# Attention with a running sum moved from PSUM to SBUF, and a third PSUM bank for the scores

## The chip, the cores and the metric

One core of a Trainium2 chip runs the whole program. The metric is the device time of one execution in microseconds; lower is better. The kernel's engines are PE (TensorE), DVE (VectorE), ACT (ScalarE), POOL (GpSimd) and SP, which issues nearly all DMAs.

## What is computed

A transformer block on x of 2 x 2048 tokens with 256 channels: attention with 16 heads of 64, layer norm, a gated network of four layers with 1024 hidden channels, layer norm. The attention is what matters here; it has a normed query and key, a distance bias that a gate on each key scales, and a causal mask.

```python
q = _rmsnorm((x @ Wq).reshape(B, T, H, D), q_rms_w)      # k likewise; v without the norm
gate = softplus(einsum('bthd,hd->bht', k, u_n) / sqrt(D))
bias = -dist * omega_eff[h] * gate[:, :, None, :]        # -inf above the diagonal
scores = einsum('bihd,bjhd->bhij', q, k) / sqrt(D) + bias
y = einsum('bhij,bjhd->bihd', softmax(scores, -1), v).reshape(B, T, H * D) @ Wproj
```

## The kernel before

The attention comes first, for 32 heads (two batches of 16) in 16 pairs; the network's two stages follow and are the same in both kernels. PE multiplies float32 data as rounded float32r, and precision is kept by splitting a value into its rounded part (`_hi`) and the rest (`_lo`), with a product for each part that matters.

For one head, scores are made transposed: keys on the partitions, 512 queries (`QB`) along the columns. A unit is one such tile, 128 keys by up to 512 queries; with four blocks of queries (`qb`, a group each) and the causal mask there are `NU` = 40 units in a head, 4, 8, 12 and 16 for the four groups. For each unit:

- PE makes the scores in a bank of `ps_s` (L1089 and L1090, on the diagonal also L1092, which adds the mask). Banks are taken in turn, two of them; before it, PE waits on `ex_done` for the unit two before (L1084 and L1085).
- ACT takes the exponential out of the bank twice, rounded into `e_hi` (L757, not for whole units) and full into `e_all` (L764). `e_all` has a ring of 3 and is overwritten when POOL's rest of the unit three before is made.
- POOL makes `e_lo` = `e_all` - `e_hi` (`take_rest`, L489) for the split units ("P"); units of mode "F", 14 of the 40, are multiplied whole.
- PE multiplies with the values, two units late (`LAG`; L1110 for a whole unit, L1115, or L1120 and L1122, for a split one) and four units late with `e_lo` (`LAG_LO`; L1131). The output is a bank of `ps_v`, which ACT copies out at the end of a group (L773).

L1115 serves the units called merged: `kt` even and not on the diagonal, 12 in a head (2, 4 and 6 in the groups `qb` 1, 2 and 3). One matmul with 128 columns of stationary data gives the products of `e_hi` with the rounded values, the sum of the weights, and the rests of the values but for the last column's, for which there is no room. That column is made on DVE: for each merged unit it multiplies `e_hi` with the column's rests, one scalar per key, and adds to a running sum in the PSUM bank `ps_r`. L993 starts the sum, L995 goes on, L999 ends it into `last_rest` (SBUF, rounded, two buffers in turn), and once a group PE adds this with the matmul L1109 (`to_last` picks the column). DVE's L998 waits until PE is through with the group two before, that is with that buffer's reader.

Row maxima for the softmax come from a product of their own: PE writes a tile of queries by keys into one of two banks `ps_m` (L1070), 40 in a head, and DVE reduces it (L957 on the diagonal, which also adds the mask, and L960 elsewhere); PE waits for the max two before (`mx_free`). DVE also has the norms, gates and the low part of transposed queries and keys (L946); POOL has squares and the splits of weights and values.

The bank `ps_r` has a second use ahead of the sums: `work_bank` lets the projections, the root's scratch and the transposes of the first head alternate between `ps_p` and `ps_r`, and `first_bank` takes it as one of four for the first transposes of x.

The order of the work on every engine is one list, `attention_steps`, in which each helper step has a due time by hand; every engine goes through the list and executes its part of each step, in order, with semaphores between engines. Heads come in pairs, and in the steady part a pair repeats every 128 us or so.

Of the kernel before, what the change touches and what calls it, by code (L numbers as in the profile page):

```python
# [49 lines left out]
KQ_RING = 2  # L50
E_RING, HI_RING, LO_RING, Q_RING = 3, 4, 3, 3
# [222 lines left out]
def attention(nc, x, wq, wk, wv, q_rms_w, k_rms_w, omega, u, yt_dram, recip_dram, rows_dram, rest_dram, kept, w1_w, w2_w, wproj):  # L274
    ctx = ExitStack()
    with ctx:
# [19 lines left out]
        last_rest = [sb(f"last_rest{i}", [P, QB], F32R) for i in range(2)]  # L296
# [44 lines left out]
        ps_s = [pb(f"ps_s{i}") for i in range(2)]  # L341
# [3 lines left out]
        ps_r = pb("ps_r")  # L345
# [81 lines left out]
        def first_bank(j):  # L427

            return (ps_p, ps_v[0], ps_v[1], ps_r)[j % 4]

        def work_bank(step):
            return (ps_p, ps_r)[work_no[step] % 2] if work_no[step] < two_banks else ps_p
# [268 lines left out]
        def _(act):  # L701
# [6 lines left out]
            for step in steps:  # L708
# [31 lines left out]
                if step[0] == "scores":  # L740
                    n, v = step[1:]
                    u_ = NU * n + v
                    qb, kt = UNITS[v]
                    off = max(0, kt - TQ * qb) * P
                    by = bias[n % 2][:, kt, qb:qb + 1]
                    if v == 0:
                        act.wait_ge(bias_done, n + 1)
                    act.wait_ge(st_full, u_ + 1)
                    if MODES[v] != "F":
                        i = count_of("PD", u_)  # L750
                        if i >= HI_RING:
                            before = split_units[i - HI_RING]
                            act.wait_ge(pv_hi, before + 1)
                            rest_taken(act, before)
                            if merged(before % NU):
                                last_rest_taken(act, before)
                        nc.scalar.activation(e_hi[:, i % HI_RING, off:QB], ps_s[u_ % 2][:, off:QB], ACT.Exp, bias=by).then_inc(hi_done, 1)  # L757
                    if u_ >= E_RING:
                        before = u_ - E_RING
                        if MODES[before % NU] == "F":  # L760
                            act.wait_ge(pv_hi, before + 1)
                        else:
                            rest_taken(act, before)
                    nc.scalar.activation(e_all[:, u_ % E_RING, off:QB], ps_s[u_ % 2][:, off:QB], ACT.Exp, bias=by).then_inc(ex_done, 1)  # L764
# [11 lines left out]
        def _(dve):  # L776
# [70 lines left out]
            for step in steps:  # L847
# [128 lines left out]
                if step[0] == "values":  # L976
# [3 lines left out]
                    if merged(v):  # L980
# [11 lines left out]
                        if kt == 0:  # L992
                            nc.vector.tensor_scalar(ps_r[:], e_in, v_last, None, ALU.mult).then_inc(rest_part, 1)  # L993
                        elif kt < TQ * qb - 2:
                            nc.vector.scalar_tensor_tensor(ps_r[:], e_in, v_last, ps_r[:], ALU.mult, ALU.add).then_inc(rest_part, 1)  # L995
                        else:
                            if grp >= 2:
                                dve.wait_ge(pv_hi, units_before(*divmod(grp - 2, NQB)))  # L998
                            nc.vector.scalar_tensor_tensor(last_rest[grp % 2][:], e_in, v_last, ps_r[:], ALU.mult, ALU.add).then_inc(rest_part, 1)  # L999
# [11 lines left out]
        def _(pe):  # L1011
            pe.wait_ge(s_cg, IDENT_MADE)

            for step in steps:
# [57 lines left out]
                if step[0] == "scores":  # L1072
# [11 lines left out]
                    if u_ >= 2:  # L1084
                        pe.wait_ge(ex_done, u_ - 1)  # L1085
                    out = ps_s[u_ % 2][:, off:QB]
# [4 lines left out]
                    if diag:  # L1091
                        last = nc.tensor.matmul(ps_s[u_ % 2][:, off:off + P], ident_r[:], mask_kq[:], start=False, stop=True)  # L1092
                    last.then_inc(st_full, 1)
                if step[0] == "values":
# [10 lines left out]
                    if MODES[v] == "F":  # L1105
                        pe.wait_ge(ex_done, u_ + 1)
                        if qb and kt == TQ * (qb + 1) - 1:
                            last_rest_taken(pe, NU * n + max(w for w in MERGED if UNITS[w][0] == qb))
                            nc.tensor.matmul(bank[0:D, :], to_last[:], last_rest[grp % 2][:], start=False, stop=False, skip_group_check=True)  # L1109
# [780 lines left out]
```

## Time and profile before

| | us |
|---|---|
| median of 3 runs | 3277.13 (3273.59 to 3280.3) |
| the profiled execution | 3275.87, its span 3274.1 |
| PE busy in the span | 3091.7 (94%) |
| DVE busy | 1842.4 (56%) |
| ACT busy | 1840.9 (56%) |
| POOL busy | 1561.0 (48%) |
| mean granted clock of TensorE | 0.981 of full speed |

A busy time is the union of an engine's instructions; matmuls overlap each other and their ends are modelled, so PE's is not PE at its peak. The shares are over the whole span, of which the attention takes the first 2130 us or so; POOL, DVE and ACT have most of their work there. Times in the rows are from the start of the span. A row of the timeline has the start, the time taken, the engine, line, operation, output and inputs, shape and count; in brackets the idle time before it and what ended that.

### The profile page before, as it was taken

Reading aid. Unit: us, or ns where it says so; the run is one execution under the profiler, and the core shown is the slowest. Engines: PE = TensorE matmul, PEld = TensorE weight load, DVE = VectorE, ACT = ScalarE, POOL = GpSimd, SP = SyncE. Lnnn points to the kernel's source line nnn. Section 1 sums busy time; section 2 is a strip of 40 time slices with the busy share of each in tenths; the row PEclk is TensorE's granted clock in tenths of the full one; section 3 lists DMA queues with packets and bytes.
Section 4 is the critical chain, followed back from the end, with each engine's and each line's share of the span. In section 5 each row is a group of like instructions: output and inputs, shape, how many; then the busy total and the mean of one; then the engine's idle time right before and its main releaser. Section 6 shows DMA issues by size and latency. Waiting matters only on the chain. (4 is left out here: it accounts for less than half of the span.)

```text
span 3274.1 us, 46760 instructions
## 1 busy us (share of the span) xinstructions
PE 3091.7 (94%) x15184; PEld 2404.2 (73%) x15184; DVE 1842.4 (56%) x4184; ACT 1840.9 (56%) x3185; POOL 1561.0 (48%) x1355
## 2 busy tenths in 40 slices
PE   3899999999999999999999999989999999999998
PEld 3667767767667677676776776668888888788887
DVE  6577676676666776766767667653333332232323
ACT  1577777776776777777767777843332332322222
POOL 4476676676665766766766666713222320000000
PEclk7899999999999999999999999989999999999999
DMA  2332432432423324224324235344434443121110
GB/s 70 79 83 51 105 70 65 104 70 64 108 61 92 77 56 105 67 67 104 70 61 111 52 76 146 84 115 133 123 102 116 119 116 116 57 78 39 68 49 20
DMA packets 210355, 273.95 MB, mean 84 GB/s; under 512 B 68992, under 2 KB 96768, under 8 KB 209984
## 3 DMA queue, kind: packets, MB, share of 16 engines
q1 hardware_dynamic: 210112, 270.97, 32.1%
q8 instruction: 121, 1.98, 0.3%
q14 instruction: 122, 1.00, 0.1%
HBM read 97.25 MB, written 55.90 MB: 47 GB/s over the span
## 5 line engine op out<-in xcount | busy, mean ns | idle before, releaser
L489 POOL TENSOR_TENSOR e_lo<-e_all,e_hi 128x512 fp32r<-128x512 f32 (+1 forms) x832 | 1034.4, 1251 | 609.2 <-ACT e_all L764 532.4
L764 ACT ACTIVATE e_all<-ps_s,bias 128x512 f32<-128x512 f32 (+3 forms) x1280 | 786.1, 625 | 168.0 <-PE ps_s L1092 90.6
L757 ACT ACTIVATE e_hi<-ps_s,bias 128x512 fp32r<-128x512 f32 (+1 forms) x832 | 562.0, 676 | 222.5 <-PE ps_s L1090 121.4
L960 DVE TENSOR_REDUCE maxes<-ps_m 128x1 f32<-128x512 f32 x768 | 516.7, 686 | 223.7 <-PE ps_m L1070 221.3
L1070 PE MATMUL ps_m<-k_ext,q_max 128*128 128x512 f32 (+3 forms) x1280 | 460.7, 383 | 55.7 <-issue 17.0
L1089 PE MATMUL ps_s<-q_twice,k_split 128*128 128x512 f32 (+3 forms) x1280 | 485.2, 379 | 25.7 <-ACT e_all L764 20.0
L1090 PE MATMUL ps_s<-q_ext,k_ext 128*128 128x512 f32 (+3 forms) x1280 | 468.9, 366 | 0.0
L1131 PE MATMUL ps_v<-e_lo,v_both 128*65 128x512 f32 (+1 forms) x832 | 432.9, 520 | 21.3 <-POOL e_lo L489 21.3
L1070 PEld LDWEIGHTS ps_m<-k_ext,q_max 128*128 128x128 f32 x1280 | 244.7, 192 | 222.5 <-DVE maxes L957 58.5
L957 DVE CUSTOM_DVE_ANT_0 ps_m<-ps_m,mask_row 128x128 f32<-128x128 f32 (+3 forms) x512 | 253.3, 495 | 245.7 <-PE ps_m L1070 244.1
L1110 PE MATMUL ps_v<-e_all,v_full 128*65 128x512 f32 (+2 forms) x896 | 325.2, 445 | 0.0
L1089 PEld LDWEIGHTS ps_s<-q_twice,k_split 128*128 128x128 f32 x1280 | 242.2, 189 | 107.2 <-ACT e_all L764 73.3
L1090 PEld LDWEIGHTS ps_s<-q_ext,k_ext 128*128 128x128 f32 x1280 | 242.7, 190 | 26.9
L1701 POOL TENSOR_TENSOR dn_rs<-dn_rs,dn_power 128x4 f32<-128x4 f32 x8 | 8.1, 1008 | 461.4 <-DVE dn_rs L1792 461.4
L1732 ACT ACTIVATE dn_gelu<-dn_h,dn_scale 128x512 f32<-128x512 f32 x64 | 44.1, 690 | 321.5 <-PE dn_h L1830 321.5
L727 ACT ACTIVATE raw<-ps_p 128x386 f32<-128x386 f32 x248 | 122.5, 494 | 162.8 <-PE ps_p L1046 161.8
L1415 ACT ACTIVATE gelu<-up_h,up_scale 128x512 f32<-128x512 f32 x64 | 44.1, 689 | 294.9 <-PE up_h L1582 294.9
L1770 DVE TENSOR_TENSOR b_lo<-dn_gelu,b_hi 128x512 fp32r<-128x512 f32 x64 | 44.3, 693 | 288.1 <-ACT b_hi L1736 288.1
L1830 PE MATMUL dn_h<-a_lo,h_hi 128*128 128x512 f32 x512 | 204.2, 399 | 0.0
L1830 PE MATMUL dn_h<-a_hi,h_lo 128*128 128x512 f32 x512 | 204.0, 398 | 0.0
L1582 PE MATMUL up_h<-p_hi,h_hi 128*128 128x512 f32 x512 | 201.8, 394 | 1.4 <-DVE h_lo L1445 1.4
L1830 PE MATMUL dn_h<-a_hi,h_hi 128*128 128x512 f32 x512 | 202.6, 396 | 0.3 <-DVE a_lo L1763 0.3
(230 smaller groups left out, 6569.1 us busy)
## 6 DMA issues: line engine op xcount, KB each, us to landing
q_twice<-q_max SPq DMA_DIRECT2D x256, 128.0 KB, 2.4
yt<-y_out SPq DMA_DIRECT2D x128, 130.0 KB
k_ext<-kq_hi SPq DMA_DIRECT2D x128, 128.0 KB, 2.3
q_max<-kq_hi SPq DMA_DIRECT2D x128, 128.0 KB, 2.4
k_split<-kq_hi SPq DMA_DIRECT2D x128, 128.0 KB, 2.4
k_split<-kq_lo SPq DMA_DIRECT2D x128, 128.0 KB, 2.4
q_ext<-kq_lo SPq DMA_DIRECT2D x128, 128.0 KB, 2.4
hidden<-gelu SPq DMA_DIRECT2D x64, 256.0 KB, 2.1
```

Source lines behind the costliest of these rows:

```text
L489: on.tensor_tensor(e_lo[:, i % LO_RING, off:QB], e_all[:, u_ % E_RING, off:QB], e_hi[:, i % HI_RING, off:QB].bitcast(F32), ALU.subtract).t ...
L757: nc.scalar.activation(e_hi[:, i % HI_RING, off:QB], ps_s[u_ % 2][:, off:QB], ACT.Exp, bias=by).then_inc(hi_done, 1)
L764: nc.scalar.activation(e_all[:, u_ % E_RING, off:QB], ps_s[u_ % 2][:, off:QB], ACT.Exp, bias=by).then_inc(ex_done, 1)
L957: nc.vector.tensor_tensor_reduce(ps_m[m % 2][:, 0:width], ps_m[m % 2][:, 0:width], mask_row[:, QB - width:QB], 1.0, NEG, ALU.add, ALU.max, ...
L960: nc.vector.tensor_reduce(maxes[:, qt, kc:kc + 1], ps_m[m % 2][:, 0:width], AX.X, ALU.max).then_inc(mx_free, 1)
L1070: nc.tensor.matmul(ps_m[m % 2][:, 0:width], q_max[s][:, qt * P:(qt + 1) * P], k_ext[s][:, kc * QB:kc * QB + width], start=True, stop=True) ...
L1089: nc.tensor.matmul(out, k_split[s][:, k], q_twice[grp % Q_RING][:, off:QB], start=True, stop=False)
L1090: last = nc.tensor.matmul(out, k_ext[s][:, k], q_ext[s][:, q], start=False, stop=not diag)
L1110: nc.tensor.matmul(bank[0:V_REST, off:QB], v_full[s][:, kt // TQ, kt % TQ - TQ // 2, 0:V_REST], e_all[:, u_ % E_RING, off:QB], start=False ...
L1131: nc.tensor.matmul(ps_v[(n * NQB + qb) % 2][0:V_REST, off:QB], v_both[s][:, kt, 0:V_REST], e_lo[:, i % LO_RING, off:QB], start=False, stop ...
L1582: last = nc.tensor.matmul(ps_h[o % 2][:], w[:, k, col], p[:, k, :], start=k == 0 and j == 0, stop=k == OC - 1 and j == 2)
L1830: last = nc.tensor.matmul(ps_h[o % 2][:], w[:, k, col], p[:, k, :], start=k == 0 and j == 0, stop=k == OC - 1 and j == 2)
```

## The change

The running sum is in SBUF (`rest_acc`, float32), its last step goes into a single `last_rest`, and the wait ahead of this step is for the group before instead of two before. The PSUM bank that comes free is the third of `ps_s`: `S_RING` = 3, and the scores of a unit wait for the exponential three before. The first uses of `ps_r` as a work bank are now those of `ps_s[2]`, and the scores of unit 2, which take that bank first, wait once for the last turn of head 0.

```diff
+S_RING = 3
-        last_rest = [sb(f"last_rest{i}", [P, QB], F32R) for i in range(2)]
+        rest_acc = sb("rest_acc", [P, QB])
+        last_rest = sb("last_rest", [P, QB], F32R)
-        ps_s = [pb(f"ps_s{i}") for i in range(2)]
+        ps_s = [pb(f"ps_s{i}") for i in range(S_RING)]
-        ps_r = pb("ps_r")
...
-            return (ps_p, ps_r)[work_no[step] % 2] if work_no[step] < two_banks else ps_p
+            return (ps_p, ps_s[2])[work_no[step] % 2] if work_no[step] < two_banks else ps_p
...
                         if kt == 0:
-                            nc.vector.tensor_scalar(ps_r[:], e_in, v_last, None, ALU.mult).then_inc(rest_part, 1)
+                            nc.vector.tensor_scalar(rest_acc[:], e_in, v_last, None, ALU.mult).then_inc(rest_part, 1)
                         elif kt < TQ * qb - 2:
-                            nc.vector.scalar_tensor_tensor(ps_r[:], e_in, v_last, ps_r[:], ALU.mult, ALU.add).then_inc(rest_part, 1)
+                            nc.vector.scalar_tensor_tensor(rest_acc[:], e_in, v_last, rest_acc[:], ALU.mult, ALU.add).then_inc(rest_part, 1)
                         else:
-                            if grp >= 2:
-                                dve.wait_ge(pv_hi, units_before(*divmod(grp - 2, NQB)))
-                            nc.vector.scalar_tensor_tensor(last_rest[grp % 2][:], e_in, v_last, ps_r[:], ALU.mult, ALU.add).then_inc(rest_part, 1)
+                            dve.wait_ge(pv_hi, units_before(*divmod(grp - 1, NQB)))
+                            nc.vector.scalar_tensor_tensor(last_rest[:], e_in, v_last, rest_acc[:], ALU.mult, ALU.add).then_inc(rest_part, 1)
...
-                    if u_ >= 2:
-                        pe.wait_ge(ex_done, u_ - 1)
-                    out = ps_s[u_ % 2][:, off:QB]
+                    if u_ == 2:
+
+                        pe.wait_ge(tr_free, NTURN)
+                    if u_ >= S_RING:
+                        pe.wait_ge(ex_done, u_ + 1 - S_RING)
+                    out = ps_s[u_ % S_RING][:, off:QB]
...
-                            nc.tensor.matmul(bank[0:D, :], to_last[:], last_rest[grp % 2][:], start=False, stop=False, skip_group_check=True)
+                            nc.tensor.matmul(bank[0:D, :], to_last[:], last_rest[:], start=False, stop=False, skip_group_check=True)
```

`first_bank`, both exponentials of ACT (L757, L764) and the mask's matmul (L1092) change in the bank they name alone.

## Rows read from the trace of the kernel before

**Rows 1.** Stretches: us, busy and count per engine, PE's clock, DMA share, GB/s.

```profile
100.00:2130.00 2030.00, 1933.48 (x9399) 1433.28 (x9398) 1398.09 (x3342) 1483.57 (x2626) 1359.38 (x1167) 0.99 0.34 81
```

**Rows 2.** Waits of PE, 100 to 2130 us: total us, times, longest.

```profile
PE ps_v L1131 <- POOL e_lo L489: 21.3, 14, 1.7
PE ps_s L1089 <- ACT e_all L764: 20.0, 49, 0.6
...
PE ps_m L1070 <- DVE maxes L957: 14.8, 17, 1.2
PE ps_m L1070 <- DVE maxes L960: 7.8, 23, 1.1
```

**Rows 3.** Waits of PE's weight loads, 100 to 2130 us, in the same columns.

```profile
PEld ps_s L1089 <- ACT e_all L764: 73.3, 135, 1.0
...
PEld ps_m L1070 <- DVE maxes L957: 54.8, 111, 1.5
...
PEld ps_m L1070 <- DVE maxes L960: 43.0, 106, 1.4
```

**Rows 4.** Timeline, 822 to 840 us: PE's waits late in a pair.

```profile
822.29 0.51 PE L1089 MATMUL ps_s<-q_twice,k_split 128*128 128x512 f32 x1 [0.43 <-ACT e_all L764]
...
836.99 0.50 PE L1089 MATMUL ps_s<-q_twice,k_split 128*128 128x512 f32 x1 [0.55 <-ACT e_all L764]
...
839.71 0.30 PE L1070 MATMUL ps_m<-k_ext,q_max 128*128 128x128 f32 x1 [1.40 <-issue]
```

**Rows 5.** Lines: ns min/median/max, first and last start, forms.

```profile
L946 DVE SCALAR_TENSOR_TENSOR kq_lo<-ps_r,qk_w,kq_hi x2: 750/750/751, 71.5 to 79.5; 128x512 fp32r<-128x512 f32 x2
...
L1089 PE MATMUL ps_s<-q_twice,k_split x1280: 219/393/767, 105.6 to 2128.3; 128*128 128x512 f32 x128, 128*128 128x384 f32 x19, 128*128 128x128 f32 x19, 128*128 128x256 f32 x17
...
L1070 PE MATMUL ps_m<-k_ext,q_max x1280: 220/393/797, 77.4 to 2088.6; 128*128 128x512 f32 x127, 128*128 128x384 f32 x20, 128*128 128x128 f32 x19, 128*128 128x256 f32 x17
```

**Rows 6.** The tile `ps_r`: DVE's sums, in the columns of rows 5.

```profile
L995 DVE SCALAR_TENSOR_TENSOR ps_r<-e_hi,v_both,ps_r x192: 712/747/755, 132.9 to 2124.9; 128x512 f32<-128x512 f32 x192
L993 DVE TENSOR_SCALAR ps_r<-e_hi,v_both x96: 673/747/754, 116.1 to 2111.7; 128x512 f32<-128x512 f32 x96
L999 DVE SCALAR_TENSOR_TENSOR last_rest<-e_hi,v_both,ps_r x96: 736/746/750, 119.6 to 2125.7; 128x512 fp32r<-128x512 f32 x96
```

**Rows 7.** L938 (columns of rows 5), timeline at 2285 us, lines behind 2130 us.

```profile
L938 DVE TENSOR_TENSOR bias<-away,c_all x32: 221/228/585, 70.7 to 2030.4; 128x64 f32<-128x64 f32 x32
...
2284.77 1.30 POOL L1353 TENSOR_TENSOR y_in<-y_in,y_rest 128x512 f32<-128x512 f32 x1 [2.45 <-DMA r_in<-recip_sums]
2285.38 1.23 DVE L1450 TENSOR_TENSOR y_lo<-y_in,y_hi 128x512 fp32r<-128x512 f32 x1 [1.91 <-ACT y_hi L1385]
2286.15 1.62 POOL L1355 TENSOR_TENSOR y_in<-y_in,r_in 128x512 f32<-128x512 f32 x1
...
L1450 DVE TENSOR_TENSOR y_lo<-up_y_first,y_hi 128x512 fp32r<-128x512 f32 x8 | 5.5, 682 | 0.0
```

**Rows 8.** Timeline, 755 to 864 us: sums on DVE, and `e_lo` on POOL.

```profile
755.16 0.74 DVE L999 SCALAR_TENSOR_TENSOR last_rest<-e_hi,v_both,ps_r 128x512 fp32r<-128x512 f32 x1
...
804.72 2.56 POOL L489 TENSOR_TENSOR e_lo<-e_all,e_hi 128x512 fp32r<-128x512 f32 x2
...
806.11 0.75 DVE L995 SCALAR_TENSOR_TENSOR ps_r<-e_hi,v_both,ps_r 128x512 f32<-128x512 f32 x1
...
863.95 0.74 DVE L999 SCALAR_TENSOR_TENSOR last_rest<-e_hi,v_both,ps_r 128x512 fp32r<-128x512 f32 x1
```

**Rows 9.** A wait of ACT, 100 to 2130 us, in the columns of rows 2.

```profile
ACT e_all L764 <- POOL e_lo L489: 69.1, 56, 3.7
```

**Rows 10.** Lines of DVE behind 2130 us: busy us, mean ns; idle before.

```profile
L1779 DVE TENSOR_TENSOR dn_y<-dn_o,dn_scale_out 128x256 f32<-128x256 f32 x32 | 13.6, 423 | 19.5 <-PE dn_o L1842 19.5
L1795 DVE TENSOR_SCALAR dn_y<-dn_y,dn_mean_var,dn_rs 128x256 f32<-128x256 f32 x32 | 11.1, 408 | 9.1 <-POOL dn_rs L1701 9.1
```

**Rows 11.** A stretch behind the wait at 839.71, in the columns of rows 1.

```profile
840.00:844.00 4.00, 4.00 (x16) 2.66 (x15) 1.57 (x6) 1.74 (x3) 1.60 (x3) 0.57 0.77 174
```

More of the change, by code:

```diff
@@ L427, in first_bank @@
         def first_bank(j):
-            return (ps_p, ps_v[0], ps_v[1], ps_r)[j % 4]
+            return (ps_p, ps_v[0], ps_v[1], ps_s[2])[j % 4]
         def work_bank(step):
-            return (ps_p, ps_r)[work_no[step] % 2] if work_no[step] < two_banks else ps_p
+            return (ps_p, ps_s[2])[work_no[step] % 2] if work_no[step] < two_banks else ps_p
         def work_free(eng, step):
@@ L756, in _ @@
                                 last_rest_taken(act, before)
-                        nc.scalar.activation(e_hi[:, i % HI_RING, off:QB], ps_s[u_ % 2][:, off:QB], ACT.Exp, bias=by).then_inc(hi_done, 1)
+                        nc.scalar.activation(e_hi[:, i % HI_RING, off:QB], ps_s[u_ % S_RING][:, off:QB], ACT.Exp, bias=by).then_inc(hi_done, 1)
                     if u_ >= E_RING:
@@ L763, in _ @@
                             rest_taken(act, before)
-                    nc.scalar.activation(e_all[:, u_ % E_RING, off:QB], ps_s[u_ % 2][:, off:QB], ACT.Exp, bias=by).then_inc(ex_done, 1)
+                    nc.scalar.activation(e_all[:, u_ % E_RING, off:QB], ps_s[u_ % S_RING][:, off:QB], ACT.Exp, bias=by).then_inc(ex_done, 1)
                 if step[0] == "take":
@@ L1091, in _ @@
                     if diag:
-                        last = nc.tensor.matmul(ps_s[u_ % 2][:, off:off + P], ident_r[:], mask_kq[:], start=False, stop=True)
+                        last = nc.tensor.matmul(ps_s[u_ % S_RING][:, off:off + P], ident_r[:], mask_kq[:], start=False, stop=True)
                     last.then_inc(st_full, 1)
```

## The prediction

> **What bounds the kernel now.** I read the stretches first: the attention part runs from about 100 to 2130 us and is the only part whose instructions the change touches; there PE is busy 1933 of 2030 us, ACT 1484, DVE 1398, POOL 1359 [rows 1]. So PE carries the time, and it has little idle time to give. Next the waits of PE in that stretch, since nothing but these can be won or lengthened: 21.3 us for POOL's `e_lo`, 20.0 us for ACT's `e_all` at the scores' matmul, 22.6 us (14.8 and 7.8) for DVE's maxes [rows 2]. The weight loads run ahead of the matmuls and show how often PE comes near a wait: 135 loads of the scores wait for ACT, 217 loads of the maxes (111 and 106 of 1280) for DVE [rows 3]. The kernel is thus a PE program whose three feeders are nearly as full as it is, DVE (0.69 busy) as a feeder of the maxes no less than ACT of the scores.
>
> **The third bank of scores.** It moves one wait: the matmul of unit u needs `e_all` of unit u-3 and no longer of u-2. What it can give is the 20.0 us in 49 waits of [rows 2], the longest 0.6 us. Behind the scores of u, PE goes to the values of u-2; for a split unit these want only `e_hi`, which ACT finished one activation (0.69 us) before `e_all`, and for a whole unit the scores' own 0.6 us of matmuls cover the wait. So nearly each of these waits goes. What is late next decides what is kept. In the pair of heads between 710 and 840 us the trace has scores' waits of 0.43 us at 822.29 and 0.55 us at 836.99; the latter is followed 2.7 us on by 1.40 us of idle before the first max of the next head, 839.71, and that is after a chain of DMAs on SP which the bank doesn't move [rows 4]. The place repeats once in each pair, and what is won there is lost to that wait. It is 0.55 of some 1.4 us in a pair (with two smaller waits of about 0.2 us that I count from the starts of matmuls), 40%. Kept: 0.6 x 20 = 12 us. If the ends of all the waits are kept it is 20, if the feeders take all back it is 0.
>
> **The new wait for `tr_free` (unit 2, once) and the bank's second use.** The bank also serves projections, transposes and scratch up to the last turn of head 0, as `ps_r` did. DVE's last reader of it in that role starts at 79.5 us and takes 0.75; the first scores' matmul starts at 105.6 [rows 5]. Behind this wait on PE stands everything, but it is over 25 us before. Zero.
>
> **One `last_rest` and not two.** DVE now waits for `pv_hi` of the group before instead of two before. Queued behind it on DVE are the maxes. But the sum's last step also waits for `hi_done` of its own unit, whose scores PE issues behind the values of the three units before, the group's end among them. PE runs in order, so the new wait is over when the old one is. Zero; an upper bound is one L1109 matmul a group, which lies beside work already issued.
>
> **The running sum in SBUF.** The instructions stay: 192 at L995, 96 at L999 and 96 at L993, each about 0.746 us with the sum in PSUM [rows 6]. What changes is where operands lie. L995 and L999 read `e_hi` and now `rest_acc`, both in SBUF. The trace has DVE instructions of that kind. L938 (two SBUF inputs, 128x64) takes 221 ns at least and 228 in the middle, but 585 at most, though its work is always the same. L1450 shows why: the one at 2285.38 starts 0.69 us before POOL's L1353 (2284.77 + 1.30) ends and takes 1.23 us, where the mean of the same operation on the first block, without POOL at work, is 0.682. POOL's next, begun in that time, takes 1.62 where L1353 of the same size takes 1.30 [rows 7]. So an instruction of DVE with two SBUF inputs, and one of POOL, don't run together: the later one stands until the earlier is through. With r us of POOL's instruction left, 1.23 - 0.68 = 0.55 is added for r = 0.69: the extra is r - 0.14. With its sum in PSUM, L995 takes 0.75 us even there, as at 806.11 inside POOL's `e_lo` work that lasts to 807.28 [rows 8].
> The Trainium skill, SBUF — State Buffer, section Who interferes with whom, states this: VectorE's second input comes through a read interface that it shares with GpSimd, and who issues second is blocked for the whole instruction. By that rule the trace agrees, with the 0.55 and 0.32 us above. It speaks against this change.
>
> How often: POOL is busy 0.67 of the stretch [rows 1]. In one pair of heads 18 such instructions start, the first at 755.16 and the last at 863.95 [rows 8]. I laid each start against POOL's instructions: 10 begin with more than 0.14 us left of one, and r - 0.14 sums to 4.1 us (the largest 1.03, that at 806.11). Sixteen pairs give 65 us more of DVE. The ends: 0 if the exclusion were not to hold for this operation, and 95 us if starts were random (288 x 0.67 x 0.5). I take 65, the direct count. Of this DVE has 632 us idle in 2030, but the maxes stand behind these instructions, in order, and PE has only two `ps_m` banks. I compared each max's end with the start of the matmul that takes its bank next (1280 of them, 77.4 to 2088.6 us [rows 5]): a sixth begin at once, 53 to 55 ns after it, and a third within 0.5 us. A delay of some 0.4 us at those places goes through: a third of 65, 22 us on PE (ends: 0 and 45).
> POOL the other way: an instruction of POOL that would begin while such an addition runs stands until it is through. By the same count, with 0.14 us taken off each, it is 46 us over the stretch. PE takes `e_lo` four units late, so it rarely notices, but ACT waits for `e_lo` before it overwrites `e_all`, 69.1 us in 56 waits now [rows 9]. I take a sixth of the 46 as reaching PE, 8 us (ends: 0 and 25; the third bank is what keeps ACT's delay off PE).
>
> L993 is a tensor_scalar with one SBUF input; L1795, of this kind and in SBUF, takes 408 ns for 256 columns, L1779, with an input in PSUM, 423 [rows 10]. So it neither gets faster by much nor has a second input: 0, between -2 and +14 us (the extra count for its 96 starts is 35 to 40 us of DVE, a third on PE).
> The Trainium skill, VectorE: DVE Perf Modes, section Mode 2×_2P, has fp32 tensor_scalar in SBUF at two elements a cycle over both ports. By that rule L993 would be some 0.27 us shorter and would exclude POOL as well; the row of 408 ns speaks against it, and it would change the sum by less than 10 us.
>
> **Sum.** -12 (scores) + 22 (maxes) + 8 (`e_lo` by way of ACT) = +18; waits that fall together (the wait for SP's chain at each head's start among them) take about a fifth of what is added, 6: +12 to +14, say 14. The span is 3274.1 in an execution of 3275.87, 1.8 us around it; 3275.9 + 14 = 3290. The median of the three runs is 3277.13, 1.3 above the profiled one, well within their spread.
>
> **Rivals.**
> (a) The delays stay in DVE's and POOL's idle time and the bank's gain is kept: 3276 - 12 = 3264. For it: DVE idle 31%, a max's slack is over 0.5 us in two of three cases, PE waited for `e_hi` or POOL seldom. Against: the additions sit where DVE is already queued (at half of them the next DVE instruction follows without idle time). It decides if under a sixth of the 65 us arrives.
> (b) Gain and loss cancel: 3271 to 3283, if a fifth of the delays arrive.
> [...]
> (d) That the change doesn't do what it says: the single `last_rest` orders groups after all. One matmul of 0.4 us for 96 groups, 38 us; excluded by PE's order, so it has no chance of its own.
>
> **How the numbers follow.** Forecast (own range 3279 to 3305) 0.45, (a) 0.17, (b) 0.22, (c) 0.16. Predicted 3290. Range 3264 to 3320. What a measurement can tell is 0.2%, 6.5 us: faster 0.17, same 0.23 (b and the low edge of the forecast), slower 0.60.
>
> **What would show it.** L995 and L999 with a maximum near 2 us and a mean near 0.97 (0.746 + 65/288); L993 at 0.69 to 0.75. PE's waits for `e_all` at the scores near zero; those for DVE's maxes up from 22.6 to 40 or more; ACT's for `e_lo` up from 69; L489 with a mean above 1.25. If L995 stays at 0.75 the exclusion step is wrong and (a) holds. If L995 grows but the maxes' waits don't, the third that I pass on to PE is wrong. If the waits for `e_all` come back at the values of u-2, the bank's gain is.

## The result and the profile after

| | before | after |
|---|---|---|
| median, us | 3276.02 (3273.59 to 3280.3), 4 runs | 3308.14 (3302.11 to 3311.25), 4 runs |
| profiled execution, us | 3275.87 | 3307.72, its span 3305.9 |
| mean granted clock | 0.981 | 0.982 |

The ratio is 1.0096, 95% interval 1.0083 to 1.0108: slower by 32 us, where 14 were forecast.

The page's busy times, and the stretches up to and behind the attention, after:

```profile
PE 3091.2 (94%) x15184; PEld 2409.9 (73%) x15184; DVE 1915.1 (58%) x4184; ACT 1834.6 (55%) x3185; POOL 1617.4 (49%) x1355
...
100.00:2162.00 2062.00, 1931.98 (x9398) 1438.36 (x9397) 1468.50 (x3339) 1478.17 (x2627) 1414.14 (x1166) 0.99 0.34 80
2162.00:3306.00 1144.00, 1113.12 (x5616) 936.00 (x5616) 376.51 (x687) 339.40 (x528) 161.99 (x123) 0.98 0.30 89
```

PE and ACT work as long as before; DVE is busy 73 us more and POOL 56. All of the 32 us lie in the attention, which answers to [rows 1]: its stretch is 2062 us and not 2030, at the same clock of 0.99; what is behind it takes 1144 us in both kernels.

PE's waits in that stretch, after (total us, times, longest):

```profile
PE ps_m L1070 <- issue: 26.5, 13, 3.2
PE ps_m L1070 <- DVE maxes L958: 23.3, 37, 1.3
PE ps_v L1134 <- POOL e_lo L490: 21.7, 15, 1.7
PE ps_m L1070 <- DVE maxes L961: 14.7, 38, 1.1
PE ps_v L1112 <- DVE last_rest L999: 12.9, 15, 0.9
PE ps_p L1057 <- issue: 9.4, 15, 0.6
PE ps_m L1070 <- DMA k_split<-kq_hi: 6.3, 2, 3.8
PE ps_v L1123 <- ACT e_hi L758: 4.2, 3, 2.7
```

Two more of PE's waits before, which the rows ahead of the prediction don't have:

```profile
PE ps_m L1070 <- issue: 17.0, 14, 2.2
...
PE ps_m L1070 <- DMA k_split<-kq_hi: 3.3, 2, 3.0
```

Laid against [rows 2], the waits for `e_all` at the scores are gone (20.0 to nothing), and in their place stand 15.4 us more for DVE's maxes (22.6 to 38.0), 9.5 more at the first max of a pair ("issue", 17.0 to 26.5), 12.9 for `last_rest`, 9.4 at the transposes L1057, 3.0 and 4.2 in the last two rows. That is 54 us of new waits against 20 given up, 34 net: the loss by name. PE's waits for POOL did not move (21.3, 21.7).

The tile of the sum after, which answers to [rows 6]; POOL's L490, whose mean was 1294 ns before; and the sum's three lines:

```profile
L996 DVE SCALAR_TENSOR_TENSOR rest_acc<-e_hi,v_both,rest_acc x192: 712/774/1770, 132.7 to 2156.3; 128x512 f32<-128x512 f32 x192
L994 DVE TENSOR_SCALAR rest_acc<-e_hi,v_both x96: 398/644/1565, 115.8 to 2138.4; 128x512 f32<-128x512 f32 x96
L999 DVE SCALAR_TENSOR_TENSOR last_rest<-e_hi,v_both,rest_acc x96: 735/1298/1748, 119.3 to 2157.2; 128x512 fp32r<-128x512 f32 x96
```
```profile
L490 POOL TENSOR_TENSOR e_lo<-e_all,e_hi 128x512 fp32r<-128x512 f32 x704 | 938.6, 1339 | 559.4 <-ACT e_all L765 505.4 <-ACT e_hi L758 31.4 <-issue 12.1
```
```profile
L996 DVE SCALAR_TENSOR_TENSOR rest_acc<-e_hi,v_both,rest_acc 128x512 f32<-128x512 f32 x192 | 166.5, 867 | 3.2 <-ACT e_hi L758 3.1
...
L999 DVE SCALAR_TENSOR_TENSOR last_rest<-e_hi,v_both,rest_acc 128x512 fp32r<-128x512 f32 x96 | 109.7, 1143 | 4.1 <-ACT e_hi L758 2.1
L994 DVE TENSOR_SCALAR rest_acc<-e_hi,v_both 128x512 f32<-128x512 f32 x96 | 74.4, 775 | 3.9 <-ACT e_hi L758 3.9
```

The rest of POOL's 56 us is in its splits and squares, L692 above all (1097 ns before, 1287 after). In PSUM no sum took over 0.755 us. In SBUF L996 averages 0.867 and L999 1.143: (867 - 746) x 192 + (1143 - 746) x 96 = 61 us more. The lines' means hide how it happens; the timeline of the changed kernel shows a case in both directions:

```profile
836.82 1.04 POOL L689 TENSOR_TENSOR v_both<-raw,one 128x512 fp32r<-128x512 f32 x1
...
837.00 1.41 DVE L999 SCALAR_TENSOR_TENSOR last_rest<-e_hi,v_both,rest_acc 128x512 fp32r<-128x512 f32 x1
...
838.00 1.55 POOL L490 TENSOR_TENSOR e_lo<-e_all,e_hi 128x512 fp32r<-128x512 f32 x1
```

POOL's L689 ends at 837.86, with 0.86 us left when L999 starts; by the prediction's r - 0.14 L999 would take 0.745 + 0.86 - 0.14 = 1.47, and it took 1.41: 0.20 less than the two together. It ends at 838.41, 0.41 after POOL's L490 starts, and that takes 1.55 where its undisturbed neighbours take 1.28: 0.27 more, which is 0.41 less 0.14. By the Trainium skill, SBUF — State Buffer, section Who interferes with whom, the port pair that VectorE shares with GpSimd is one exclusive lock; the trace agrees, with these two numbers. Below, this exclusion is called the lock.

It holds for every one. I laid each start against the other engine's instructions, over the whole trace of the changed kernel. Of the 288 L996 and L999, 113 start with 0.14 us or less left of a POOL instruction, and none of these takes over 0.752 us; the 175 others average 1.097, and each is within 0.05 us of 0.746 + r - 0.20. In the kernel before, 159 of the 288 start with as much of POOL's left, and average 0.744. The other way, 175 POOL instructions of 128x512 (L490, L692, L677, L694) start with over 0.10 us left of a sum and take r - 0.14 more than the same line undisturbed, 60 us in all.

### The profile page after: what moved, and what is told of

It reads as the page before. It is cut to its first block and busy times, and to the rows that moved or that the text cites. A ratio compares the mean times of both kernels' runs of the same rounds, so it can differ in the third digit from the quotient of the medians.

```text
span 3305.9 us, 46760 instructions
## 1 busy us (share of the span) xinstructions
PE 3091.2 (94%) x15184; PEld 2409.9 (73%) x15184; DVE 1915.1 (58%) x4184; ACT 1834.6 (55%) x3185; POOL 1617.4 (49%) x1355
## 5 line engine op out<-in xcount | busy, mean ns | idle before, releaser
L490 POOL TENSOR_TENSOR e_lo<-e_all,e_hi 128x512 fp32r<-128x512 f32 (+1 forms) x832 | 1064.5, 1289 | 582.0 <-ACT e_all L765 510.0
L1070 PE MATMUL ps_m<-k_ext,q_max 128*128 128x512 f32 (+3 forms) x1280 | 468.5, 387 | 83.1 <-issue 26.5
L1092 PE MATMUL ps_s<-q_twice,k_split 128*128 128x512 f32 (+3 forms) x1280 | 477.7, 373 | 4.2 <-DMA q_twice<-q_max 4.2
L1134 PE MATMUL ps_v<-e_lo,v_both 128*65 128x512 f32 (+1 forms) x832 | 432.1, 519 | 21.7 <-POOL e_lo L490 21.7
L1092 PEld LDWEIGHTS ps_s<-q_twice,k_split 128*128 128x128 f32 x1280 | 242.6, 190 | 49.4 <-issue 12.9
```

What stands on the lines that cost most here:

```text
L490: on.tensor_tensor(e_lo[:, i % LO_RING, off:QB], e_all[:, u_ % E_RING, off:QB], e_hi[:, i % HI_RING, off:QB].bitcast(F32), ALU.subtract).t ...
L1070: nc.tensor.matmul(ps_m[m % 2][:, 0:width], q_max[s][:, qt * P:(qt + 1) * P], k_ext[s][:, kc * QB:kc * QB + width], start=True, stop=True) ...
L1092: nc.tensor.matmul(out, k_split[s][:, k], q_twice[grp % Q_RING][:, off:QB], start=True, stop=False)
L1134: nc.tensor.matmul(ps_v[(n * NQB + qb) % 2][0:V_REST, off:QB], v_both[s][:, kt, 0:V_REST], e_lo[:, i % LO_RING, off:QB], start=False, stop ...
```

## The experiments

**The parts apart.** Three kernels: the sum in SBUF with the scores' two banks (the freed bank unused but as a work bank); and, to have the third bank without the exclusion, the 384 steps of the sum as maxima over `e_hi`, with one input, in three banks and in two; these two leave the sum out.

```diff
# e1_sbuf_2banks, against after
-S_RING = 3
+S_RING = 2
# e2_nolock_3banks, against after; e3_nolock_2banks is the same with S_RING = 2
-    nc.vector.tensor_scalar(rest_acc[:], e_in, v_last, None, ALU.mult)
-    nc.vector.scalar_tensor_tensor(rest_acc[:], e_in, v_last, rest_acc[:], ALU.mult, ALU.add)
-    nc.vector.scalar_tensor_tensor(last_rest[:], e_in, v_last, rest_acc[:], ALU.mult, ALU.add)
+    nc.vector.tensor_reduce(rest_max[:], e_in, AX.X, ALU.max)    # in each of the three places
```

> The changed kernel with two banks of scores and not three: the running sum stays in SBUF and last_rest single, and the eighth PSUM bank is the first work bank only. If the loss is all the sum's (DVE and POOL excluding each other) and the third bank gave some 12 to 20 us, this is slower than the changed kernel (3308) by as much: 3320 to 3328. If the third bank itself costs time (PE further ahead, other queues late), it is faster than 3308. Waits of PE for e_all at the scores come back to 20 us or more.

> The changed kernel, but each of DVE's 384 steps of the last column's sum is a maximum over e_hi's 512 columns (one SBUF input, one result per partition), so the sum is left out and last_rest stays zero; order, waits and the 96 matmuls stay. One such reduction takes 0.686 us in the trace against 0.745, so DVE has 22 us less of work than before. Theory of the exclusion: no instruction of the sum now takes longer while POOL works, and the third bank's gain is bare, 3256 to 3264. Rival, that the third bank or the single last_rest costs: 3276 or more. PE's wait for last_rest, 12.9 us in the changed kernel, goes under the first and stays under the second.

> The same with two banks of scores, the control for e2: the sum is left out in the same way. Theory of the exclusion: near the kernel before, 3270 to 3276 (DVE has 22 us less of work, a third of which may reach PE). The difference to e2 is what the third bank gives without the sum's cost: 12 us by my sum, 20 if all waits for e_all are kept, 0 if what is late next takes it back.

| kernel | us | ratio to before |
|---|---|---|
| e1, SBUF sum, 2 banks | 3311.1 (3308.08 to 3312.94) | 1.0105 [1.0092, 1.0118] |
| after, SBUF sum, 3 banks | 3308.14 | 1.0096 [1.0083, 1.0108] |
| e3, no sum, 2 banks | 3267.76 (3263.48 to 3268.19) | 0.9972 [0.9961, 0.9983] |
| e2, no sum, 3 banks | 3263.81 (3261.84 to 3276.16) | 0.9966 [0.9955, 0.9978] |

The bank gives 3 us with the sum in SBUF (e1 to after) and 4 without it (e3 to e2), about what the ranges can tell from nothing; 12 were forecast, and the 3320 to 3328 expected of e1 was missed with it. In e11 and e12 below, with another order of the maxes, three banks are 3 us slower than two, with ranges that overlap. The sum in SBUF costs 34 us against the sum in PSUM (before to e1). Against the reductions it is 43, but these are also 0.07 us shorter each (e3 came out 2 us under its expected 3270 to 3276).

PE's waits in e3 and in e2 (whose profiled execution was its longest, 3276.16):

```profile
PE ps_s L1092 <- ACT e_all L768: 20.1, 49, 0.6
PE ps_m L1073 <- DVE maxes L961: 14.7, 17, 1.2
PE ps_m L1073 <- issue: 12.1, 13, 2.0
```
```profile
PE ps_m L1072 <- issue: 27.9, 14, 3.0
PE ps_v L1136 <- POOL e_lo L491: 21.5, 15, 1.7
PE ps_m L1072 <- DVE maxes L960: 17.2, 16, 1.3
PE ps_p L1059 <- issue: 9.1, 15, 0.6
```

The bank takes away the 20.1 us wait for wait, and with no sum at all the waits "issue" at the pair's first max (12.1 to 27.9) and at the transposes L1059 (9.1, new) come up in the same way as in the changed kernel. (e7 below, which is e2 with small memsets, has 32.7 and 9.2 there in an execution at its median, so that this isn't e2's long execution.) But the sum in SBUF brings both up too, with two banks. e1's waits:

```profile
PE ps_m L1071 <- issue: 25.4, 15, 3.9
PE ps_m L1071 <- DVE maxes L959: 21.5, 42, 1.2
...
PE ps_m L1071 <- DVE maxes L962: 13.8, 37, 1.1
PE ps_p L1058 <- issue: 7.9, 14, 0.6
```

So these two waits show either cause, a PE that comes earlier or a DVE that comes later, and don't tell them apart. The growth of the maxes' waits belongs to the sum in SBUF: 35.3 us in e1, against 22.6 before, 21.7 in e3 and 24.5 in e2. The wait for `last_rest` needs both: e1 and e2 have none, the changed kernel 12.9, and e8 below 13.0. With the bank, ACT too waits for DVE's sums to release `e_hi`: 21.4 us in the changed kernel, 4.7 before and in e1.

**Where in a pair it happens.** A pair has 80 units. I laid the starts of the scores of two traces against each other and took the difference gained in each ten units, mean of 13 pairs, us a pair:

| | units 0 to 30 | 30 to 40 | 40 to 50 | 50 to 60 | 60 to 70 | 70 to 80 | x16 |
|---|---|---|---|---|---|---|---|
| before to e1 (lock) | 0.04 | 0.72 | 0.00 | 0.12 | 1.02 | 0.24 | 34 |
| e1 to after (bank) | -0.01 | 0.00 | -0.93 | 0.57 | 0.03 | 0.01 | -5 |
| e3 to e7 (bank, no sum) | 0.02 | 0.00 | -0.88 | 0.07 | 0.82 | 0.24 | 4 |
| before to e16 (below) | 1.49 | -0.55 | -0.35 | -0.06 | -1.77 | -0.08 | -21 |
| the sums' own growth, before to e1 | 0.91 | 0.97 | -0.27 | 1.80 | 1.06 | 0.16 | 74 |
| share of time DVE is busy, before | 0.55 | 0.94 | 0.92 | 0.79 | 0.66 | 0.83 | |

The bank wins 0.93 us a pair, 15 in 16 pairs, at the units 40 to 50, and gives most back at once; without the sum it gives all back at 60 to 80. The lock costs nothing where half a pair's time lies (units 0 to 30, 60 us of 128), though the first 10 units hold 0.93 of the 4.6 us that its sums grow by in a pair; it costs at units 30 to 40 and 60 to 70. In the kernel before, unit 30 starts at 799.4 in the pair shown (unit 0 at 739.9), unit 40 at 813.0, 60 at 837.0 and 70 at 854.6. Its stretches say why for the first of these (us, busy and count of PE, PEld, DVE, ACT, POOL):

```profile
776.00:784.00 8.00, 8.00 (x42) 6.62 (x41) 3.69 (x8) 4.82 (x10) 4.60 (x5) 1.00 0.01 1
...
800.00:808.00 8.00, 7.76 (x34) 5.09 (x33) 7.73 (x18) 6.33 (x10) 7.52 (x7) 1.00 0.01 1
...
824.00:832.00 8.00, 7.85 (x40) 5.12 (x38) 7.52 (x23) 6.94 (x14) 6.66 (x6) 1.00 0.09 22
```

DVE, 0.69 busy on the average, is 3.69 of 8 us busy at 776 and 7.2 to 7.7 of 8 in each stretch from 800 to 832, where also the norms and gates of the next pair are on it. It is PE's equal there: of the 0.97 us that the sums grow by at units 30 to 40, 0.72 arrive. But the largest growth, 1.80 at 50 to 60, arrives there with 0.12 only, and 1.02 come at 60 to 70, where DVE is 0.66 busy and PE waits for the pair's first max. That the one is handed on to the other, by the chain below, is read from the trace and not tested. A stretch of the changed kernel, with DVE and POOL full:

```profile
812.00:820.00 8.00, 7.67 (x34) 4.74 (x32) 8.00 (x16) 5.94 (x10) 8.00 (x8) 1.00 0.00 0
```

And PE's waiting place behind the bank's gain is DVE's as well. The timeline of before at the pair's end:

```profile
830.59 0.31 DVE L931 STREAM_TRANSPOSE bias_out<-bias_in 128x128 f32<-128x128 f32 x1
...
831.00 0.63 PE L1057 MATMUL ps_p<-ident,raw 128*128 128x128 f32 x4
...
836.50 0.48 SPq L545 DMA_DIRECT2D k_ext<-bias_rows  x1
```

PE's transposes start 0.10 us behind the end of DVE's `bias_out` in each of the 15 pairs, and in the changed kernel too; that is in the units 50 to 60. From there PE, ACT, DVE and SP's DMAs lead to the first max at 839.71 [rows 4], in the units 60 to 70. A PE that comes earlier by the bank waits for DVE, at L1057 (9.4 us) and at the first max; a DVE that comes later by the lock makes it wait at the same two places (e1).

**How much of added time arrives.** The kernel without the sum and with three banks (e2) was loaded: e6 puts a small reduction ahead of each middle and last step on DVE, with no second input; e7 a memset on POOL ahead of each merged unit's `e_lo`.

```diff
# e6_dve_longer, against e2: middle step; last step (0:300)
+    nc.vector.tensor_reduce(fill[:], e_in[:, 0:16], AX.X, ALU.max)
# e7_pool_longer, against e2
+    nc.gpsimd.memset(fill[:], 0.0).then_inc(fill_done, 1)
```

> As e2_nolock_3banks (the sum left out, each step a maximum of e_hi, 0.68 us), but a small maximum over 16 columns goes ahead of each middle step (192, some 0.18 us) and one over 300 columns ahead of each last step (96, some 0.45 us): DVE has about 78 us more work, as much as the exclusion adds to it in the changed kernel, and nothing of it excludes POOL. Theory that DVE's lateness is the cost: 3264 + 25 to 35, 3289 to 3299, with PE's waits for DVE's maxes as in the changed kernel. Rival, that POOL's standing is the cost (or both halves): 3264 to 3280.

> As e2_nolock_3banks, but ahead of each merged unit's e_lo POOL has a small memset (384 of 0.10 us, with the wait between them some 0.12 to 0.15): POOL has 40 to 56 us more, as in the changed kernel, and DVE none. Theory that DVE is what costs: 3264 to 3270. Rival, POOL by way of ACT: 3275 to 3290, with ACT's wait for e_lo well over 80 us.

e6: 3291.87 (3289.0 to 3295.77), ratio 1.0052 [1.004, 1.0065]. The kernel is 28 us longer, with no exclusion at work. DVE's busy time is 1869.4 us against 1831.3 in e2, 38 more, but the new records overlap their neighbours; from each one's start to the next instruction's it is 14 + 36 = 51 us. So between a half and three quarters of it arrive. The maxes' waits don't grow by it (23.8 us, 24.5 in e2), against what I expected; PE waits 8.0 us for the last step instead. e7: 3270.51 (3265.57 to 3276.14, 11 runs), 0.9983 [0.9974, 0.9992]: 7 us longer, with intervals that still overlap. It was a weak test: 384 memsets of 0.10 us made POOL only 14 us busier (1574.7 and 1560.8, where 40 to 56 were meant), and 257 of them are followed by idle time of POOL. What POOL's delays cost in the lock stays open.

**Which of the sums.** e8 keeps L999 alone as it is, the rest are reductions; e15 makes L994 alone a reduction; e5 gives L994 a second multiply, by a column of ones, meant to keep it off the second port.

```diff
# e5_ts_one_port, against after
-    nc.vector.tensor_scalar(rest_acc[:], e_in, v_last, None, ALU.mult)
+    nc.vector.tensor_scalar(rest_acc[:], e_in, v_last, one[:, 0:1], ALU.mult, ALU.mult)
```

> The changed kernel with only the last step of each group's sum as it is (96, two SBUF inputs, mean 1143 ns in the changed kernel against 743 before); the 288 others are maxima of e_hi, so the sum is left out but for its last term. The last steps carry 38 of some 70 us that the exclusion adds to DVE, and the PE waits for last_rest 12.9 us. If the cost goes by DVE's added time, it is a half or more of 44: 3284 to 3292. If the places matter (the last step stands ahead of maxes that PE waits for), up to 3300. If the middle and first steps are what costs, under 3275.

> The changed kernel with the sum's first step (96 times, L994, mean 775 ns in the changed kernel, maximum 1565) as a maximum of e_hi, 0.68 us and no two-port form; the sum lacks its first term. If this step excludes POOL in its two-port form as the others do with their second input, the kernel gets faster by more than its 0.09 us x 96 = 9 us of DVE time, 8 to 15 us with what POOL stood: 3293 to 3300. If it costs nothing, as the prediction had it, 3305 to 3309.

> The changed kernel, but the sum's first step (96 times, L994) gets a second multiplication, by a column of ones, so that it has two pointer scalars as L1795 has, which took 408 ns for 256 columns. In the changed kernel this step took 398 ns at least, and up to 1565. If the two-port form is what makes it exclude POOL, it now takes some 0.69 us throughout, never over 0.76, and the kernel gets faster: of 775 - 690 = 85 ns x 96 = 8 us less on DVE and less standing on POOL, 5 to 12 us, 3296 to 3303. If the exclusion is only that of instructions with two SBUF inputs, the maximum was something else and the time stays at 3305 to 3311.

e8: 3280.12 (3278.33 to 3286.46, 11 runs), 1.0021 [1.0012, 1.003]: 16 us over e2, so the 96 last steps are over a third of the lock's 43; that is less than the 3284 to 3292 expected. e15: 3305.39 (3296.03 to 3305.94), 1.0079 [1.0066, 1.0092], 3 us under the changed kernel with intervals that overlap, where I had written 3305 to 3309 for a step that costs nothing: L994 is in the lock, but its price at the end is not told from zero. e5: 3307.35 (3304.97 to 3314.08), 1.0101 [1.0087, 1.0115]. It told nothing apart, since L994 kept its short form and its spread:

```profile
L994 DVE TENSOR_SCALAR rest_acc<-e_hi,v_both,one x96: 459/644/1565, 116.1 to 2142.8; 128x512 f32<-128x512 f32 x96
```

**The wait for `last_rest`.** e4 moves the matmul that adds it behind the group's last `e_lo` matmul, two units on.

```diff
# e4_late_last, against after
-                            last_rest_taken(pe, ...)      # ahead of the last whole unit's values
-                            nc.tensor.matmul(bank[0:D, :], to_last[:], last_rest[:], ...)
...
+                    if qb and kt - TQ * qb == TQ // 2 - 1:      # behind the group's last e_lo
+                        last_rest_taken(pe, ...)
+                        last = nc.tensor.matmul(..., to_last[:], last_rest[:], ...)
```

> The changed kernel with one thing moved: the matmul that adds last_rest goes behind the last e_lo matmul of its group instead of ahead of the last whole unit's, some 1.2 us later in PE's order, and DVE's wait for its reader is on that matmul. If PE's 12.9 us of waits for last_rest are a loss of their own, it takes 8 to 13 us off the changed kernel: 3295 to 3300. If they stand in for a wait that follows anyway (the first max of the next head), the time stays at 3305 to 3308.

3305.22 (3303.11 to 3307.94), 1.0088 [1.0075, 1.0101]; its waits:

```profile
PE ps_p L1057 <- DVE bias_out L932: 16.0, 15, 1.1
PE ps_v L1135 <- DVE last_rest L999: 5.7, 15, 0.4
```

7 us of the wait for `last_rest` go and 7 us more stand at the transposes: 15 times, once a pair, for `bias_out` by name. The wait was where PE met DVE's queue first, not what it cost.

**Is it the first max?** The waits "issue" of a pair's first max suggested that the bank's gain ends in the chain to it. Four kernels start the first head's maxes later, which takes that wait away.

```diff
# e9 on after, e10 on before, e11 on e2, e12 on e3
-            start, end = (turns[0] + 0.13, t0 + 0.24) if s == 0 else (t0 + 0.27, t0 + 1.08)
+            start, end = (turns[0] + 0.17, t0 + 0.24) if s == 0 else (t0 + 0.27, t0 + 1.08)
```

> The changed kernel with one due time changed: the maxes of the first head of each pair start 0.17 of a head behind its first turn and not 0.13 (some 2.5 us later in the order of the work), so that PE has other work while DVE's last step of the gates, the transposes, ACT's copy and SP's transfers of that head get through. In all kernels so far the first transposes of a pair start 0.10 us after DVE's bias_out, and PE stands before the pair's first max, 20 us in sum in the kernel before, 33 in the changed one. Theory that DVE's delays and the third bank's gain both end at that max: 3308 less 15 to 30, 3278 to 3293. Rival, that the waits for maxes and last_rest elsewhere carry the loss: 3303 to 3310.

> The kernel before with the same due time changed. By the theory that the head of each pair waits on the chain from DVE's gates by way of SP's transfers, it gains most of the 20 us that PE stands there: 3260 to 3268, faster than both kernels. If the maxes, now closer together, make PE wait for DVE instead, 3272 to 3280.

> e2_nolock_3banks (the sum left out) with the same due time changed. If the wait before the pair's first max is where the third bank's gain was given back, the gain shows against e12: 3264 less 20 to 30, 3234 to 3246.

> e3_nolock_2banks (the sum left out) with the same due time changed: 3268 less 12 to 17, 3251 to 3256. The distance to e11 is the third bank's gain where nothing takes it back: 12 to 20 us by the prediction's sum, 4 as between e3 and e2 if the gain is lost elsewhere.

e9: 3308.24 (3307.39 to 3309.09), 1.0096 [1.0081, 1.0112]; e10: 3287.55 (3285.25 to 3292.0), 1.0037 [1.0025, 1.005]; e11: 3279.44 (3274.41 to 3283.11, 11 runs), 1.0011 [1.0002, 1.002]; e12: 3276.28 (3273.35 to 3282.33, 11 runs), 1.0004 [0.9995, 1.0013]. The wait goes in all four, and not one is faster: 0, 11, 16 and 9 us the other way. More waits stand at the maxes instead (42.2 us in e10, 22.6 before). The first max is a place where waiting shows, not what sets the pair. That theory fell.

**DVE's full stretch, relieved.** What is left is DVE's queue itself between 800 and 832. The second head's maxes can be spread to end earlier, at 0.98 or 0.88 of a head's time and not 1.08, so that fewer of them stand in it.

```diff
# e13 (0.98) and e16 (0.88) on before, e14 (0.98) and e17 (0.88) on after
-            start, end = (turns[0] + 0.13, t0 + 0.24) if s == 0 else (t0 + 0.27, t0 + 1.08)
+            start, end = (turns[0] + 0.13, t0 + 0.24) if s == 0 else (t0 + 0.27, t0 + 0.88)
```

> The kernel before with one due time changed: the 40 maxes of a pair's second head end at 0.98 of a head and not at 1.08, so some four maxes of each pair leave the stretch of units 30 to 50, in which DVE is nearly always busy, for the one ahead of it, where it is half idle. PE's work is the same, only its order. Theory that this stretch is DVE's: 4 x 0.69 us less in it for each of 16 pairs, of which a half or more is kept: 3276 less 15 to 40, 3236 to 3261. Rival, that PE or SP's transfers set the pair: 3270 to 3282.

> The changed kernel with the same due time. Theory that the loss comes in through DVE's full stretch: it gains at least what e13 gains, and more if instructions of the sum find POOL free more often: 3308 less 20 to 45, 3263 to 3288. If the loss is not in that stretch, its distance to e13 stays 32 us.

> As e13 with the maxes ending at 0.88: eight of a pair leave the full stretch. Theory: more than e13 as long as DVE has room ahead, 3225 to 3255; it turns when the stretch ahead, in which PE has no idle time, makes PE wait for maxes instead, 3255 to 3275.

> The changed kernel with the second head's maxes of a pair spread to end at 0.88 of its first turn instead of 1.08, the order that made the kernel before faster. Theory (the added VectorE time stands 1:1 wherever VectorE is full, and the lock's price depends on which sum steps meet GpSimd): it stays at least 40 us above the kernel before with the same edit (3258), at 3298 to 3320. Rival (what the order gives, it gives to the changed kernel too, and the same edit at 0.98 only hit a bad place): about 19 us below the changed kernel, 3285 to 3292.

| kernel | us | ratio to before |
|---|---|---|
| e13, before, 0.98 | 3265.2 (3263.77 to 3265.23) | 0.9962 [0.9949, 0.9974] |
| e16, before, 0.88 | 3258.05 (3255.68 to 3260.67) | 0.9943 [0.9929, 0.9956] |
| e14, after, 0.98 | 3317.47 (3316.91 to 3317.64) | 1.0123 [1.0109, 1.0137] |
| e17, after, 0.88 | 3282.96 (3280.21 to 3287.25, 8 runs) | 1.0024 [1.0013, 1.0035] |

On the kernel before the maxes alone, moved, give 11 and 18 us: no instruction is shorter, DVE's queue is only emptied before the pair's end. It is less than expected: e13 is above its 3236 to 3261, e16 above its 3225 to 3255 and within the 3255 to 3275 that I had written for an order that makes PE wait earlier. The table by units above has e16: it gives 1.5 us to units 0 to 30, where the maxes went, and gets 1.77 back at 60 to 70. Its timeline at a pair's end:

```profile
822.33 0.31 DVE L931 STREAM_TRANSPOSE bias_out<-bias_in 128x128 f32<-128x128 f32 x1
824.55 0.60 PE L1057 MATMUL ps_p<-ident,raw 128*128 128x128 f32 x4
```

The transposes start 1.91 us behind `bias_out` and no longer 0.10 (1.9 to 2.5 in the 15 pairs): DVE is not what they wait for. DVE's busy share at units 50 to 60 is 0.61 there, and 0.79 before. This is the version that beats both kernels.

On the changed kernel the same edit goes both ways: e14 is 9 us slower, where a gain of 20 or more was expected, and e17 25 us faster, where the theory had 3298 to 3320 and its rival, that the changed kernel gains as the one before does, 3285 to 3292. The rival came nearest. Laid against each other by units, e17 wins 2.7 us a pair on e14 at units 30 to 40, and gives 0.8 at units 10 to 30. At units 30 to 40 the sums of e14 take 1.8 us a pair more than in PSUM, those of the changed kernel 1.0; but those of e17 take 1.6 and it is fast. So the place is shown, and that an order's price under the lock depends on how the sums fall against POOL is argued from these; the single cause of e14's loss is open. (The mean granted clock was 0.956 in e14's profiled execution and 0.977 to 0.980 in its three others, at the same time within 1 us, so the clock isn't it.)

e17 stands 25 us above e16, where the changed kernel stands 32 above the one before: with DVE's stretch relieved the change still loses, and loses less, though its sums take more extra time in a pair (5.9 us against 4.0).

## Why the prediction was right and wrong

**Right: that the exclusion decides.** What [rows 7] show on one pair of instructions behind the attention held in all 288 sums, with 0.20 in place of 0.14 on DVE's side and 0.14 on POOL's: L996 and L999 predicted at a mean near 0.97, measured (166.5 + 109.7) / 288 = 0.959; 65 us forecast, 61 measured; a maximum near 2 us, 1.77. POOL's forecast was 46 us, its busy time rose by 56. The maxes' waits rose to 38.0 (40 or more forecast), and ACT's for `e_lo` from 69.1 to 81.1:

```profile
ACT e_all L765 <- POOL e_lo L490: 81.1, 40, 3.7
```

The sign "L489 with a mean above 1.25" told nothing: it was 1.294 before the change, and is 1.339.

Right as well: `tr_free` costs nothing, the scores' waits for `e_all` go and don't come back at the values, and DVE doesn't wait at L999 for the single `last_rest`: its own waits there are 2.1 us, for `e_hi`, where before had 2.7. Rival (a) and (b) fell with the interval. No run shows a loss by the clock, which the 0.16 for (c) and the upper end of 3320 would need: it is 0.99 over the stretch in both kernels. In the kernel before it fell behind the 1.40 us of idle at 839.71 and stayed at full speed behind 1.65 us at 1871.7.

**Wrong: the bank's 12 us; it gives 3.** The step that failed is "Kept: 0.6 x 20 = 12". I looked for what is late next at one place, in one pair, as it stood with the bank not yet there: 0.55 us of 1.4 lost to the first max. The bank wins the 15 us that the sum needed and loses them within 20 units, since PE then stands where DVE's queue, by `last_rest` (12.9 us) and `bias_out`, is late. The 0.10 us between `bias_out` and the transposes was in the trace of before, in all pairs but the first (0.06 there). I had read the chain from SP's DMAs on, one step too late. This is 9 of the 18 us that the forecast was short.

**Wrong: "a third" of DVE's 65 us, a sixth of POOL's 46, and a fifth less for overlap.** Forecast 22 + 8, less 4 to 6: some 25; measured 34 (before to e1). This is the other 9 of the 18 us. I took one share of tight maxes over all 1280; counted again, a tenth of them (by the matmuls' starts) or a fifth (by their weight loads') begin at once, and 27% or 36% within 0.5 us, so the count was about right. But over time it isn't one share: next to none of the extra arrives at units 0 to 30; of the other 3.7 us a pair in e1 (60 in all) 34 arrive. (In e6 0.42 us a pair arrive in the first ten units as well, so these are not free for every load.) The 69% that DVE is busy is a mean over 46% at 776 us and 93% from 800 to 832, and [rows 1] as one stretch hid it. The deduction for overlap had no row behind it. How the 34 divide between DVE's and POOL's delays isn't settled. The sums of e1 grow by 75 us in all, and e6's share, a half to three quarters, would make 38 to 56 of that, so DVE's lateness is enough for the whole; whether POOL's 60 us add anything is open, since no run held one of them fixed with the lock in place.

**Right in size, wrong in reason: L993.** I took it as neither shorter nor locked, from the 408 ns of L1795 for 256 columns [rows 10]. In SBUF its 512 columns take 398 to 489 ns, 445 on the average, in the 33 cases that start with 0.14 us or less left of a POOL instruction, and 948 in the 63 others, up to 1565: alone it is over a third shorter, and it is in the lock as well. The mean, 775 against 737, makes 4 us in 96, within the bounds that I gave. By the Trainium skill, VectorE: DVE Perf Modes, section Mode 2×_2P, fp32 tensor_scalar in SBUF runs at two elements a cycle over both read ports, and I had let [rows 10] speak against that; the trace of the changed kernel agrees with the page. Why L1795 takes 403 to 416 ns for half the columns in each of its 32 cases is open: it has another operation, a subtract and a multiply with two factors per partition, and was a poor witness for L993.

**Not foreseen: PE's wait for `last_rest`.** 12.9 us in 15 waits. I had looked at the single buffer, which costs nothing, and not at L999 being late by 0.4 us on the average at the group's end. By e4 it is a place and not a price.

## What to carry to other kernels

Here an operand moved from PSUM to SBUF put a two-input VectorE operation into exclusion with GpSimd, and both paid; the added time of each could be counted in the trace of before, start by start (65 us counted, 61 measured). What of it reaches the end is read in stretches of a few us over one period of the loop, not from the mean over all: here a helper that is busy 69% in all is nearly full for a quarter of the period, and from there on over half of what was added arrived (34 of 60 us), while a buffer that freed TensorE from another helper mostly brought it there sooner. Before adding buffers, try to move the full helper's deferrable work out of that stretch: here that alone gave 18 us.

## What the runs showed of the hardware that was not expected

- A tensor_scalar of 128x512 float32, SBUF to SBUF, with its factor per partition: 398 to 489 ns where 0.14 us or less is left of a POOL instruction, against 737 on the average into PSUM; with a second factor per partition 459 at least (e5). Both reach 1565 beside POOL.
- In the exclusion the later instruction takes its own time plus nearly all that is left of the other, r: on DVE r - 0.20 (175 scalar_tensor_tensor of the changed kernel, all within 0.05 us), on POOL r - 0.14 (175 tensor_tensor; one of 1.28 us that began with 0.41 us of L999 left took 1.55).
- With one of the two inputs in PSUM there is none of it: 159 sums that began beside a POOL instruction average 0.744 us, the 129 others 0.745.
- A mean granted clock of 0.956 in one execution of a kernel and 0.977 to 0.980 in three others (e14) left its time the same within 1 us.
